# A graph network on one core: five small words per block for TensorE, and the last layer's projections handed to VectorE

## The reference

```
x, src, dst, edge_attr : 50,000 nodes of 128 values, 50,000 edges (dst sorted), 64 values per edge
h = x
for _ in range(3):                                     # three layers, same weights
    msgs = relu(h[src] @ W_edge + b_edge)
    agg  = segment_sum(msgs, dst, 50000)
    h    = relu(concat(agg, h) @ W_agg + b_agg)
x1 = layernorm(x + h)
q, k, v = x1 @ Wq + bq, x1 @ Wk + bk, x1 @ Wv + bv     # then attention over the edges,
conv = attention(q, k, v, edge_attr @ We) + x1 @ Wskip + bskip
...                                                    # a feed-forward block, and layernorms
```

## Time and profile before

| | |
|---|---|
| median of three runs | 4414.99 us (4407.94 to 4415.50) |
| profiled execution, own time | 4418.77 us |
| its span | 4416.8 us |
| TensorE busy | 3870.5 us, 88% |
| VectorE busy | 3504.8 us, 79% |
| ScalarE busy | 2212.4 us, 50% |
| GpSimd busy | 2904.4 us, 66% |
| mean granted TensorE clock | 0.952 |
| message passing, first to last gather, both layers | 599.5 to 1679.5 us |
| last layer, first gather to last projection eviction | 1732.2 to 2506.5 us |

### The profile page before, as it was taken

One profiled execution on the slowest core, in us unless ns is written; L12 is line 12 of the kernel. 1 busy time (PEld: TensorE's weight loads), 2 busy tenths in 40 slices (PEclk: granted clock), 3 DMA queues, 4 the chain that ended last, 5 costly groups with the idle time before them and its releaser, 6 DMA issues. The chain is left out here.

```text
span 4416.8 us, 106271 instructions
## 1 busy us (share of the span) xinstructions
PE 3870.5 (88%) x21528; PEld 2665.2 (60%) x21627; DVE 3504.8 (79%) x11629; ACT 2212.4 (50%) x4904; POOL 2904.4 (66%) x2864
## 2 busy tenths in 40 slices
PE   5777769999899997999999788888888869999998
PEld 3555548888788886566666466666666634444443
DVE  6888857766566665788777689999999958999998
ACT  1333335555455553455444444444444437777776
POOL 3777757776477773655554177777777667777775
PEclk9999979999999998999999889999998879999999
DMA  2555558877678775788888667777777534444443
GB/s 86 175 175 175 175 158 244 246 237 234 185 239 243 238 232 176 267 303 299 295 294 277 237 192 207 208 208 209 206 208 206 170 99 120 131 124 126 130 124 93
DMA packets 610107, 878.32 MB, mean 199 GB/s; under 512 B 148009, under 2 KB 409232, under 8 KB 609932
## 3 DMA queue, kind: packets, MB, share of 16 engines
q1 hardware_dynamic: 490764, 631.93, 43.7%
q0 software_dynamic: 119168, 244.63, 21.3%
HBM read 477.60 MB, written 398.61 MB: 198 GB/s over the span
## 5 line engine op out<-in xcount | busy, mean ns | idle before, releaser
L798 POOL DMA_INDIRECT mp_gathered<-msg_rows,other_idx x784 | 755.9, 964 | 348.6 <-issue 192.5
L1120 POOL DMA_INDIRECT ll_gathered<-msg_rows,other_idx x392 | 382.7, 976 | 361.1 <-PE bank L1138 204.6
L816 PE MATMUL bank<-mp_edge_hot,mp_gathered 128*128 128x256 bf16 x3528 | 477.7, 276 | 33.9 <-POOLq L786 19.4
L560 POOL DMA_INDIRECT by_window<-so_pay,so_pos_i x392 | 387.5, 988 | 165.9 <-issue 111.6
L1713 POOL DMA_INDIRECT ff_agg<-at_rows,last_idx x392 | 385.8, 984 | 116.0 <-issue 102.6
L1417 POOL DMA_INDIRECT at_q<-kvq_rows,node_idx x392 | 376.9, 961 | 119.4 <-issue 119.1
L1415 POOL DMA_INDIRECT at_kv<-kvq_rows,kv_idx x392 | 374.2, 955 | 119.6 <-issue 111.4
L872 ACT ACTIVATE mp_h_out<-bank,mp_b_agg 128x256 f32<-128x256 f32 x392 | 185.6, 474 | 480.1 <-PE bank L834 476.8
L816 PEld LDWEIGHTS bank<-mp_edge_hot,mp_gathered 128*128 x3528 | 347.3, 98 | 104.6 <-issue 61.0
L905 DVE TENSOR_SCALAR mp_edge_hot<-digits,mp_first_col,column 128x256 bf16<-128x256 bf16 x1176 | 340.8, 357 | 65.2 <-issue 53.1
L1833 PE MATMUL bank<-ff_gelu,ff_w 128*128 128x512 f32 x784 | 378.4, 605 | 1.2 <-ACT ff_gelu L1865 1.2
(11 more groups left out here) (267 smaller groups left out, 9493.5 us busy)
## 6 DMA issues: line engine op xcount, KB each, us to landing
msg_rows<-mp_msg_out SPq DMA_DIRECT2D x392, 192.0 KB
kvq_rows<-ll_proj SPq DMA_DIRECT2D x98, 768.0 KB
mp_h_in<-h_cols SPq DMA_DIRECT2D x392, 128.0 KB
h_cols<-mp_h_out SPq DMA_DIRECT2D x392, 128.0 KB
msg_rows<-so_msg_out SPq DMA_DIRECT2D x98, 384.0 KB
h_cols<-so_h_out SPq DMA_DIRECT2D x98, 256.0 KB
ll_h_in<-h_cols SPq DMA_DIRECT2D x196, 128.0 KB
x_rows<-ll_x_b SPq DMA_DIRECT2D x98, 256.0 KB
```

The costliest lines, as they stand in the source:

```text
L560: pool.indirect_dma_start(core.by_window, bass.IndirectOffsetOnAxis(ap=pos_i[k][:, t:t + 1], axis=0), pay[k][:, t, :], None, bounds_check= ...
L798: pool.indirect_dma_start(gathered[:, r * PARTS * D:(r + 1) * PARTS * D], None, core.msg_rows[layer % 2], bass.IndirectOffsetOnAxis(ap=cor ...
L816: product = nc.tensor.matmul(agg_bank[k], gathered[:, bass.ds(at + d * D, D)], hot, start=(first and d == 0), stop=True, skip_group_check= ...
L1120: pool.indirect_dma_start(gathered[:, r * PARTS * D:(r + 1) * PARTS * D], None, core.msg_rows[(LAYERS - 1) % 2], bass.IndirectOffsetOnAxis ...
```

## The change

Five words per block replace one. A new table `tile_words` holds for each block the slots of its three tiles, the count of tiles to wait for and the number of further tiles; VectorE makes it in `window_tables`. TensorE loads 20 of these words at every fourth block, in both stages. VectorE goes on reading `spans`. The waits of TensorE in message passing get one common value per block, `at`, with the head starts of three semaphores set so that they fit (`H_HEAD`, `U_HEAD`, `REST_HEAD`), and the wait on h ahead of the tiles goes; `tile_in` becomes one semaphore per layer.

In the last layer all four projection tiles get their biases from VectorE, and the ones-products, the ScalarE evictions and the bias split go. SyncE's `store` becomes two: rows and columns keep their step, and the projections are stored at the step of the next group, behind that group's rows and columns.

```diff
@@ window_tables, VectorE
+            words = core.tile_words[:, :].rearrange("a (n k) -> a n k", k=WORDS)
+            nc.vector.tensor_scalar(at_i[:, :], core.spans[0:1, 0:NW], 511, None, ALU.bitwise_and).then_inc(words_c, 1)
+            nc.vector.tensor_scalar(final_i[:, :], core.spans[0:1, 0:NW], 9, None, ALU.logical_shift_right).then_inc(words_c, 1)
...
+            for c in range(ALWAYS):
+                nc.vector.tensor_scalar(words[:, :, c], slot_i[c][:, :], TILES - 1, None, ALU.bitwise_and)
+            nc.vector.tensor_scalar(words[:, :, ALWAYS + 1], more_f[:, :], 0.0, None, ALU.max)
@@ message_passing and last_layer, TensorE
+        def tile_words(eng, n, r):
+            if r % AHEAD == 0:
+                words[eng.engine, "tiles"] = nc.values_load_multi_w_load_instructions(
+                    core.tile_words[0:1, bass.ds(n * WORDS, AHEAD * WORDS)], engines=[eng.engine], min_val=0, max_val=NT,
...
+            word = words[eng.engine, "tiles"][r % AHEAD * WORDS:(r % AHEAD + 1) * WORDS]
+            slots = [nc.s_assert_within(x, 0, TILES - 1, ...) for x in word[:ALWAYS]]
+            return slots, eng.snap(word[ALWAYS] & 511), word[ALWAYS + 1]
@@ message_passing, TensorE
-                        at = (i & (TILES - 1)) * (PARTS * D)
+                        at = slot * (PARTS * D)
...
-                        first, final = edge_tiles(pe, n, r)
-                        reached(pe, h_ok, wins + n - 1)
-                        pe.wait_ge(edge_hot_ok, wins + n + 1)
-                        pe.wait_ge(tile_in, layer * NT + first + ALWAYS)
+                        slots, reach, count = tile_words(pe, n, r)
...
+                        pe.wait_ge(edge_hot_ok, at)
+                        pe.wait_ge(tile_in[layer], reach)
                         for c in range(ALWAYS):
-                            added = add_tile(r % 2, first + c, edge_hot[r % HOTS][:, c, :], first=c == 0)
+                            added = add_tile(r % 2, slots[c], edge_hot[r % HOTS][:, c, :], first=c == 0)
...
-                        pe.wait_ge(u_ok, wins + n + 1)
-                        reached(pe, rest_ok, wins + n - 1)
+                        pe.wait_ge(u_ok, at)
+                        pe.wait_ge(rest_ok, at)
@@ last_layer, SyncE
-            def store(g):
+            def store_x1(g):
                 k = g % 2
                 reached(sp, xb2_ok, g + 1)
                 sp.dma_start(rows(core.x1_rows, g), x1_b2[k][:, :, :]).then_inc(st_x1[k], 16)
                 reached(sp, cols_ok, g + 1)
                 sp.dma_start(core.x1_cols[:, g * GR:(g + 1) * GR], x1_cols[k][:, :]).then_inc(st_cols[k], 16)
-                reached(sp, by_act, BY_ACT * (g + 1))
-                reached(sp, by_dve, (T - BY_ACT) * (g + 1))
+
+            def store_projections(g):
+                k = g % 2
+                reached(sp, by_dve, T * (g + 1))
                 sp.dma_start(rows(core.kvq_rows, g), proj[k][:, :, :]).then_inc(st[k], 16)
...
                 if n % 2 and 0 <= n // 2 - 5 < NG:
-                    store(n // 2 - 5)
+                    store_x1(n // 2 - 5)
+                if n % 2 and 0 <= n // 2 - 6 < NG:
+                    store_projections(n // 2 - 6)
@@ last_layer, TensorE (project)
                 for t in range(T):
-                    if t < T - BY_ACT:
-                        reached(pe, by_dve, (T - BY_ACT) * (g - 1) + t + 1)
-                    else:
-                        reached(pe, by_act, BY_ACT * (g - 1) + t - (T - BY_ACT) + 1)
-                        nc.tensor.matmul(proj_bank[t][:, 0:NPJ], core.ones[0:PARTS, :], proj_parts[:, :], start=True, stop=True, skip_group_check=True)
+                    reached(pe, by_dve, T * (g - 1) + t + 1)
@@ last_layer, ScalarE
-            def evict(g, q, j):
-                reached(act, st[q % 2], 16 * (2 * j + q // 2))
-                for t in range(T - BY_ACT, T):
-                    act.wait_ge(mm, T * g + t + 1)
-                    nc.scalar.activation(proj[q % 2][:, t, :], proj_bank[t][:, 0:NPJ], ACT.Copy).then_inc(by_act, 1)
@@ last_layer, VectorE
             def add_biases(g, q, j):
                 reached(dve, st[q % 2], 16 * (2 * j + q // 2))
-                for t in range(T - BY_ACT):
+                for t in range(T):
                     dve.wait_ge(mm, T * g + t + 1)
```

More of the change, by code:

```diff
@@ L3 @@
 from contextlib import ExitStack
+from functools import partial
 F32 = mybir.dt.float32
@@ L37 @@
 ALWAYS = 3
+WORDS = ALWAYS + 2
+AHEAD = 4
 HOTS = 4
@@ L697, in message_passing, with blocks @@
         hi_ok, rest_ok, mid_ok, m_ok = core.sem("mp_hi_ready"), core.sem("mp_rest_ready"), core.sem("mp_mid_ready"), core.sem("mp_m_ready")
-        def blocks(eng, turn, ring):
+        def blocks(eng, turn, ring, count=None):
             def straight(n):
@@ L704, in do @@
                         step(n + lag, (n + lag) % ring, (n + lag) // ring)
-                turn(do)
+                turn(do) if count is None else turn(do, count + n + 1)
             for n in range(2 * RING):
@@ L730, in further, with further_tiles @@
                     more(i, (before + i - (first + (ALWAYS - 1))) & 511)
+        def tile_words(eng, n, r):
+            if r % AHEAD == 0:
+                words[eng.engine, "tiles"] = nc.values_load_multi_w_load_instructions(
+                    core.tile_words[0:1, bass.ds(n * WORDS, AHEAD * WORDS)], engines=[eng.engine], min_val=0, max_val=NT,
+                    skip_runtime_bounds_check_because="the table was made from tile numbers under NT on the chip")[1]
+            word = words[eng.engine, "tiles"][r % AHEAD * WORDS:(r % AHEAD + 1) * WORDS]
+            slots = [nc.s_assert_within(x, 0, TILES - 1, skip_runtime_bounds_check_because="the table holds five bits of it") for x in word[:ALWAYS]]
+            return slots, eng.snap(word[ALWAYS] & 511), word[ALWAYS + 1]
+        def further_tiles(eng, n, reach, count, more):
+            with eng.If(count > 0):
+                before = eng.value_load(core.more_before[0:1, bass.ds(n, 1)], min_val=0, max_val=NT - 1)
+                with eng.Fori(reach - 1, reach - 1 + count) as i:
+                    more(i, (before + i - (reach - 1)) & 511)
         with nc.Block() as block:
@@ L1089, in _ @@
                 load_x(n)
-            for n in range(NW + 14):
+            for n in range(NW + 16):
                 if n + RING - 1 < NW:
```

106 lines of the change are left out of this document (63 added, 43 removed).

## The result

The changed kernel takes **4678.23 us** (median, 4677.59 to 4683.43), the kernel before on the same chip 4415.24 us (4407.94 to 4420.21). The ratio is 1.0595, 95% interval 1.0582 to 1.0607: 6% slower, or 263 us. The forecast was 4689 us, and its range holds the measured time.

What follows compares the result with a forecast made beforehand. It took TensorE as full in both stages, its sequencer late at message-passing turns; the last layer would become bound by a loop over the projections' store. 4418.8 + 253 + 20 + 1 = 4692.8, less 3.8 to the median: 4689 us, range 4590 to 4800.

Steps and rivals of the forecast that it cites:

- the circle over the store of the projections: Last layer: y, projections issued, landed, biases, next y form a loop of 10.4 us a group against 7.56, +253 us.
- list of signs: Expected in the profile after: 10.4 us groups, VectorE waiting 2.5 to 3.5 us for the projections' store, TensorE's share near 0.63.
- Where 5.2 came from: Last layer: the projections' store lands 5.2 to 5.6 us after issue, read from where the burst's DMA share falls.
- The other engines can't shorten it.: Last layer: TensorE at 6.6 us and DMA at 6.8 us a group have room within the 10.4.
- Words in message passing: Message passing: two loads of 20 words a turn against the sequencer's gain per block, 49 turns, +20 us (-33 to +80).
- the formula: Message passing: two word loads leave TensorE dry by twice the load time less 1.55, 1.75 us a turn.
- the lead of 2.2 us: Message passing: at most 2.2 us of work can be queued ahead for TensorE by its sequencer before a word load.
- VectorE alone at 7.4 us a group: Last layer: without the wait on the projections' store, VectorE with two more biases would bound at 7.4, 0.15 below before.
- Rival 1: Last layer: the projections land within 2.6 us of issue, VectorE never waits, 4368 us; chance 0.06.
- Rival 2: Last layer: TensorE's clock falls to half as it idles, +550 us or half of it, near 4950 us; chance 0.05.
- Rival 3: Words come one by one under traffic, 3.15 us for 20, +169 in place of +20, 4838 us; chance 0.05.
- Table of words: Stage before message passing: 13 small VectorE operations, 3.3 us under an idle 3.48, +1 us at most, +3.3 without that cover.

Runs made afterwards that it cites:

- experiment 2: The kernel before with one edit, the projections stored one group later; ScalarE evictions and bias split kept: 4621.42 us, ratio 1.0470.
- experiment 1: The changed kernel with the projections stored at their old step again, VectorE keeping all four biases: 4508.78 us, ratio 1.0202.
- experiment 3: The changed kernel with four projection buffers in place of two, the late store kept: 4502.51 us, ratio 1.0187.
- experiment 4: The changed kernel with the x load, and SyncE's wait for y ahead of it, one group later: 4458.19 us, ratio 1.0087.
- experiment 7: The kernel before with the change's words, counts and waits in message passing alone, last layer as before: 4427.79 us, ratio 1.0026.
- experiment 6: The kernel before with five words a block in the last layer alone: 4433.03 us, ratio 1.0035.
- experiment 5: The changed kernel with the projections' store at its old step and TensorE back on one word a block in the last layer: 4520.12 us, ratio 1.0242.
- experiment 10: The kernel before with the x load and its wait for y one group later and all four biases on VectorE: 4466.69 us, ratio 1.0114.
- experiment 8: The kernel before with three of the four biases on VectorE in place of two: 4462.59 us, ratio 1.0105.
- experiment 11: The kernel before with the x load and its wait for y one group later and three biases on VectorE: 4445.12 us, ratio 1.0061.
- experiment 9: The kernel before with one edit, the x load and its wait for y one group later: 4408.03 us, ratio 0.9980.

## Why the prediction was right

The forecast was 4689 us (4590 to 4800) by one mechanism, the circle over the store of the projections, and the measured 4678 is that mechanism: experiment 2 makes it alone, experiments 1, 3 and 4 take it away. Two steps beside the circle were wrong or incomplete, VectorE's own bound and the words in message passing, and the forecast came near in spite of them. Step by step:

- *The circle.* Forecast 1.95 + 5.2 + 3.3 = 10.4 us a group (10.45 before rounding, which would make 257 of the 253). In the group shown it was 2.03 + 5.25 + 3.32, and 10.50 over 47 groups. The stage grew by 260 us, forecast 253. The two kinds of wait are the forecast ones, and the wait on the projections' store is 2.3 us each time (101.7 / 45), within the 2.0 to 2.7 of its working and a little under the 2.5 to 3.5 of its list of signs.
- *Where 5.2 came from.* It was taken from the end of a burst, where the DMA share falls, not from a rule; the two ends of that window are 5.25 and 5.75 after the issue, where the prediction has 5.2 to 5.6. With the traffic down from 0.90 to 0.63, the landing measured by the start of the biases was 5.25 in the group shown and 5.08 in the median.
- *"The other engines can't shorten it."* Right. With the circle open the same work takes 8.5 us a group (experiment 1), well under 10.5.
- *Words in message passing.* Forecast +20, measured +8 in the trace of the change and 12 (6 to 17) by themselves. The loads cost what was forecast; what was missing is a gain elsewhere. TensorE makes one count product per block, so the time of all 390 blocks can be compared between the traces of before and after. Leave out the blocks with further tiles first. Beyond the dense 2.51 us, the block at a load takes 1.39 more on average before, once a turn; after, the two take 0.83 and 1.08, so 1.91 a turn where the formula has 1.75. Over both layers this adds 26 us (25 in experiment 7). The 18 blocks with further tiles, with the few right behind them, take back 17 (16 in experiment 7): for these the prediction has no term. In the block shown here the step goes from 4.47 to 3.24 us, and TensorE's idle 1.16 ahead of the further tile is gone.

```profile
779.82 0.38 PE L852 MATMUL bank<-mp_lo_hot,mp_hi_hot 128*98 128x256 bf16 x2
...
783.23 0.57 PE L816 MATMUL bank<-mp_more_hot,mp_gathered 128*128 x3 [1.16 <-issue]
784.29 0.38 PE L852 MATMUL bank<-mp_lo_hot,mp_hi_hot 128*98 128x256 bf16 x2
```

```profile
781.49 0.38 PE L901 MATMUL bank<-mp_lo_hot,mp_hi_hot 128*98 128x256 bf16 x2
...
783.65 0.53 PE L860 MATMUL bank<-mp_more_hot,mp_gathered 128*128 x3
784.73 0.38 PE L901 MATMUL bank<-mp_lo_hot,mp_hi_hot 128*98 128x256 bf16 x2
```

  That the formula came so near at the loads is partly luck. The load took 1.93 us and not 1.65, and with 1.93 the formula gives 2 × 1.93 − 1.55 = 2.31 a turn. So another of its terms, the lead of 2.2 us or one of those added to the load, is off by some 0.2 us a load the other way. Which one was not tested.
- *Words in the last layer.* The prediction has no term for them. By themselves they cost 15 us (experiment 6); inside the circles they cost nothing (experiments 1 and 5: 4509 with them, 4520 without). It didn't touch the forecast, since the circle covers them.
- *VectorE alone at 7.4 us a group.* This step failed, though the forecast does not hang on it. With the stores in time a group takes 8.5, and 8.0 even with the second circle open (experiment 10). Two things were wrong in it. The x1 rows' circle was seen as 0.8 us of wait that could be subtracted; it belongs to a circle that rises by every bias put into it and takes 8.5 us with four. And VectorE's own group was put 0.6 too small: it is 8.03 with hardly a wait in it, 439.4 / 500 × 8.03 = 7.06 busy, 0.45 of waits and the rest gaps between instructions.
- *Rival 1* (the store lands in time, 4368) was thus wrong in its price as well as in its condition: landing in time gives 4503 to 4509, which is slower than before. No case of the prediction had this.
- *Rival 2* (the clock). The granted clock fell from 1.00 to 0.85 to 0.91 in the windows of the last layer, and never near half. TensorE's share was 0.73 to 0.78 (80.55 to 85.26 of 110 us) and not 0.63; how much of that is clock and how much are products stretched behind late operands was not taken apart. It did not set the end: 10.50 is the sum of the circle without any of TensorE's time, and experiment 2 has 205 us of the loss at a granted clock of 0.97. Experiment 1, where TensorE waits less, ran at 0.98.
- *Rival 3* (3.15 us a load) came true for the load in the last layer (3.55), where it is hidden, and not in message passing (1.93), where it counts. The least there is 1366 / 20 = 68 ns a word. The Trainium skill (Runtime: NRT & Kernel Launch, Instruction fetch mechanics) puts a register load at about 200 ns a register, and names it for the registers that the runtime loads; by it 20 words would be 4.0 us, an estimate (the prediction has 4.1). In message passing the trace disagrees with it as a price for the kernel's own loads, with 1.93. The last layer's 3.55 comes near to it, but there a load of eight took 1.69 on this engine and 0.60 on another, so it is no fixed price of a register here.
- *Table of words.* Nothing: message passing starts 1.2 us earlier than before, so the cover, VectorE's idle 3.48, held. It is 0.79 in the trace of after.

How the loss divides: the moved store alone is worth 205 us, and biases and words on top of it 58. With the store back in place 92 us remain. One bias by itself is 45 (experiment 8), so two are about 90 if the second costs what the first does; the words of message passing are 12 by themselves.

## What to carry to other kernels

A wait on one transfer in an in-order DMA queue times every store behind it, so before a store is moved by a step, write down after which event it will be issued and which consumer needs its buffer: if consumer and event are the same block, the landing time becomes part of the period. A wait of an engine that recurs once a group, even a short one, can be a circle close to binding and not slack: here a bias of 0.48 us put between the end of the wait and the event that releases it made the group 0.42 longer (experiment 8). Opening one circle shows the next, so price the engines' work also for the case that every such wait is gone: here that was the larger part of what the biases cost.

## What the runs showed that I had not expected

- The same load of eight words takes nearly three times as long on one engine as on another. In the kernel of experiment 5, last layer, VectorE loads them in 0.60 us and TensorE's sequencer in 1.69 (medians), beginning in the same microsecond:

```profile
L1092 DVEq TENSOR_LOAD <-spans x25: 595/599/615, 1749.4 to 2565.8; - x25
L1092 PEldq TENSOR_LOAD <-spans x25: 593/1687/2156, 1749.4 to 2567.4; - x25
```

  In message passing of the kernel before both are near 0.8 (medians 792 and 846 ns). The least is 0.59 everywhere. So it is not the traffic alone. The record of the load may hold time in which TensorE's sequencer is held up for another reason. That was not tested.
- Landings shortened little when DMA went from 0.90 to 0.63 busy. The x1 rows, where VectorE waits for them, took 3.35 us from issue to the start of `add_b2` before and 3.09 after (medians from 1900 to 2400 us); the 768 KB of projections 5.08 after, where the end of one burst before gave 5.25 to 5.75. Each moves behind the other transfers of its own burst.
- To take a ones-product, 0.37 us a group, from a TensorE that was 99% busy (experiment 11 against 9) made the group 0.38 us longer. A share of 99% did not mean that TensorE alone set the pace.
